# Attention: the third tile's exponentials move between ScalarE's two copies of the values' low rows

## What is computed

```
Q = (query @ Wq.T + bq).reshape(B, Nq, H, D).transpose(0, 2, 1, 3)
K = (key @ Wk.T + bk).reshape(B, Nkv, H, D).transpose(0, 2, 1, 3)
V = (value @ Wv.T + bv).reshape(B, Nkv, H, D).transpose(0, 2, 1, 3)
scores = jnp.einsum('bhqd,bhkd->bhqk', Q, K) * SCALE
scores = scores / temperature
attn = jax.nn.softmax(scores, axis=-1)
out = jnp.einsum('bhqk,bhkd->bhqd', attn, V)
out = out.transpose(0, 2, 1, 3).reshape(B, Nq, C)
return out @ Wo.T + bo
...
x = x + _L0_xattn_ref(_layernorm(x, axis=-1), ctx_1024, ctx_1024, ...)
x = x + _L0_ffn_ref(_layernorm(x, axis=-1), ...)
x = x + _L1_xattn_ref(_layernorm(x, axis=-1), ctx_1024, ctx_1024, ...)
x = x + _L1_ffn_ref(_layernorm(x, axis=-1), ...)
```

## Time and profile before

| | |
|---|---|
| median of 3 runs | 1826.12 us (1825.88 to 1826.61) |
| the profiled execution | 1827.0 us, of which the trace spans 1825.2 us |
| PE, DVE, ACT, POOL busy | 96%, 86%, 67%, 54% of the span |
| granted TensorE clock, mean | 0.987 |

### The profile page before, as it was taken

One profiled execution on the slowest core, in us unless ns is written; L12 is line 12 of the kernel. 1 busy time (PEld: TensorE's weight loads), 2 busy tenths in 40 slices (PEclk: granted clock), 3 DMA queues, 4 the chain that ended last, 5 costly groups with the idle time before them and its releaser, 6 DMA issues.

```text
span 1825.2 us, 29834 instructions
## 1 busy us (share of the span) xinstructions
PE 1748.5 (96%) x9082; PEld 1304.0 (71%) x9162; DVE 1563.2 (86%) x3584; ACT 1223.4 (67%) x3374; POOL 982.1 (54%) x1079
## 2 busy tenths in 40 slices
PE   8898799999999999999889999889999999999997
PEld 7786688888888888888644444457777776767775
DVE  6866789999999999988679888878888988888885
ACT  4575899999999999999533333356656655665543
POOL 2544466666666666666500000156766767767665
PEclk9999999999999999999989999999999999999999
DMA  8666445554455545544379999054445445445311
GB/s 306 201 211 186 105 124 142 153 156 139 139 153 154 146 137 157 154 117 121 93 240 389 407 395 385 26 219 171 167 151 197 161 154 197 153 163 170 124 58 41
DMA packets 153902, 322.08 MB, mean 176 GB/s; under 512 B 47376, under 2 KB 55568, under 8 KB 136080
## 3 DMA queue, kind: packets, MB, share of 16 engines
q1 hardware_dynamic: 153280, 319.38, 53.7%
q10 hardware_dynamic: 464, 0.79, 0.2%
HBM read 163.86 MB, written 105.91 MB: 148 GB/s over the span
## 4 chain that ended last, share of the span: by engine, by line
PE 45%; DVE 2%; issue 1%; ACT 1%; POOL 1%; POOLq 0%; DVEq 0%; ACTq 0%
PE f_pair L1575 12%; PE f_pair L1628 11%; PE f_pair L68 6%; PE f_pair L70 6%; PE f_pair L69 6%; PE f_pair L1615 3%; PE f_pair L1586 1%; ACT f_hf L1696 0%; DVE w L1801 0%; DVE f_st L1833 0%; POOL f_rs L1992 0%; ACT f_room L1671 0%; POOL f_ring L2020 0%; ACT f_hf L1688 0%; DVE f_x2Tl L1821 0%
## 5 line engine op out<-in xcount | busy, mean ns | idle before, releaser
L1320 POOL TENSOR_TENSOR a_pr<-a_pr,a_rcp 128x512 f32<-128x512 f32 x256 | 266.4, 1041 | 262.8 <-DVE a_rcp L1162 262.5
L1070 ACT ACTIVATE a_pr<-a_s,a_nmax 128x128 f32<-128x128 f32 x1024 | 365.4, 385 | 26.9 <-DVE a_nmax L1155 25.1
L1070 ACT ACTIVATION_READ_ACCUMULATOR a_pr<-a_s,a_nmax 128x1 f32 x1024 | 229.3, 224 | 0.0
L1575 PE MATMUL f_pair<-f_room,w 128*128 128x512 bf16 x999 | 225.2, 382 | 2.6 <-ACT f_room L1684 1.3
L1992 POOL TENSOR_TENSOR f_rs<-f_rs,f_half 128x1 f32<-128x1 f32 x128 | 121.2, 947 | 179.2 <-DVE f_rs L1839 179.2
L1793 DVE CUSTOM_DVE_ANT_0 f_hf<-f_pair,nb,sh 128x512 f32<-128x512 f32 x244 | 172.7, 748 | 29.8 <-PE f_pair L1575 29.5
L1575 PEld LDWEIGHTS f_pair<-f_room,w 128*128 128x128 bf16 x1024 | 99.6, 99 | 116.9 <-issue 3.8
L1155 DVE TENSOR_REDUCE a_nmax<-a_s 128x4 f32<-128x512 f32 x256 | 172.0, 672 | 9.6 <-PE a_s L961 7.5
L1170 DVE TENSOR_TENSOR a_pTl<-a_pt,a_pTh 128x512 fp32r<-128x512 f32 x256 | 168.5, 679 | 12.7 <-ACT a_pTh L1082 12.7
L973 PE MATMUL a_pt<-ident,a_pr 128*128 128x128 f32 x1024 | 160.7, 280 | 16.1 <-DVE a_pTl L1170 8.1
L1082 ACT ACTIVATE a_pTh<-a_pt 128x512 fp32r<-128x512 f32 x256 | 151.7, 628 | 4.5 <-PE a_pt L973 4.5
(11 more groups left out here) (443 smaller groups left out, 5091.7 us busy)
## 6 DMA issues: line engine op xcount, KB each, us to landing
hidden<-f_hf SPq DMA_DIRECT2D x57, 1024.0 KB, 8.6
f_hf<-hidden SPq DMA_DIRECT2D x57, 1024.0 KB, 4.8
xr<-x SPq DMA_DIRECT2D x96, 256.0 KB, 3.1
xb<-x SPq DMA_DIRECT2D x16, 1024.0 KB, 5.4
x<-xr SPq DMA_DIRECT2D x64, 256.0 KB, 2.3
ctxh<-bqreph SPq DMA_DIRECT2D x126, 128.0 KB, 2.4
f_room<-x SPq DMA_DIRECT2D x15, 1024.0 KB, 10.3
ctxh<-bqreph SPq DMA_DIRECT2D x128, 64.0 KB, 2.0
```

The lines of the kernel that those rows point to most:

```text
L1070: last = e.activation(pr[:, t, j, :], s_bank[t][:, j * P:j * P + P], ACT.Exp, bias=nmax[kk % 2][:, t, j:j + 1], accum_out=sums[kk % 2][:, ...
L1320: e.tensor_tensor(p, p, rcp[kk % 2][:, t, :].unsqueeze(2).to_broadcast([P, 4, KEYS]), ALU.mult).then_inc(*e_pn)
L1575: last = e.matmul(h_bank[(PAIRS * u + i) % 3][:, q, :], w1[:, k, f * P:f * P + P], xT[u % 2][:, k, :], start=k == 0, stop=k == KC - 1)
```

## The change

ACT takes the exponentials of tile 2 between the two low copies, and no longer behind both. No other engine's order changes, and no wait is added or taken away.

```diff
-            def vlow(b, kk):
+            def vlow(b, kk, i):
                 o = kk - VALUE
                 if not there(b, o):
                     return
                 u = b * TPB + o
-                for i in range(2):
-                    e_pv.wait_ge(e, 2 * u + i)
-                    e_vs.wait_ge(e, 2 * (u - 1) + i)
-                    e.activation(vl[64 * i:64 * i + 64, :], v_bank[i][64 - 64 * i:128 - 64 * i, :], ACT.Copy).then_inc(*e_vl)
+                e_pv.wait_ge(e, 2 * u + i)
+                e_vs.wait_ge(e, 2 * (u - 1) + i)
+                e.activation(vl[64 * i:64 * i + 64, :], v_bank[i][64 - 64 * i:128 - 64 * i, :], ACT.Copy).then_inc(*e_vl)
...
                 qhi(b, kk)
-                vlow(b, kk)
+                vlow(b, kk, 0)
                 exp(b, kk, 2)
+                vlow(b, kk, 1)
                 if not opening:
                     xhi(b, kk)
                 phi(b, kk, 2)
```

## The result

| | before | after |
|---|---|---|
| median of 20 runs each | 1826.0 us (1822.53 to 1829.15) | 1830.62 us (1828.55 to 1835.03) |
| profiled execution, its span | 1827.0, 1825.2 | 1828.84, 1827.0 |
| statistics step, median | 11.24 | 11.48 |
| normalising step, median | 11.24 | 11.23 |
| one of the last steps, median | 10.76 | 10.78 |

The ratio is 1.003, with a 95% interval of 1.0023 to 1.0037: the changed kernel is slower by 5.5 us (4.2 to 6.8). The lengths of steps are the distances between the first maxima of one step and of the next on DVE, worked out from the trace: medians over 24 statistics steps, 25 normalising steps and 4 of the last ones.

A forecast was written before the change was run, and what follows sets the result against it. It took a closed round through PE, ACT, DVE and POOL to bound the kernel, not PE alone. Terms 6.5 + 0.0 + 0.1 - 0.4 = +6.2 us gave 1832.3 us, forecast within 1830.5 to 1834.3, wider range 1827.5 to 1834.8.

The forecast's parts named there:

- The round: Closed round through all four engines sets the 11.24 us step; the change is worth how much `xlo`'s start moves.
- The statistics steps: 26 steps where exponentials would wait for DVE's maxima of tile 2: `xlo` 0.25 later each, 6.5 us.
- The normalising steps: 28 steps where ACT's gained 0.33 is used up by the second copy's new place: 0.00 a step.
- The last steps: Last six or so steps, without `xlo`: ACT's tile 3 exponentials start earlier, gain 0.07 a step, 0.4 in all.
- The late steps: Four steps with late queries' DMA, no gap to fill: two not already counted add 0.6, 0.5 given back, +0.1.
- Overlap for the second copy: Rival: second low copy starts 0.12 earlier, everything behind it 0.15 earlier; -2.1, 1824.0 us; chance 0.06.
- Quick hand-over: Rival: `vsum` 1 starts 0.03 behind the copy, not 0.10, in all 54 steps; +2.4, 1828.5 us; chance 0.04.
- PE the limit: Rival: PE's 96% busy share binds, the round has unseen air, the change does nothing; 1826.1 us; chance 0.05.
- Both together: Rival: second-copy overlap and 0.03 hand-over to `vsum` 1 both hold; -5.9, 1820.2 us, faster; chance 0.02.
- Worse than I say: Rival: no DMA giveback (+0.5), no last-step gain (+0.4), 0.03 more a step (+1.6); 1834.8 us; chance 0.03.
- The signs I named: Statistics step: ACT idle about 0.25, DVE about 0.35, length 11.49; normalising step stays 11.24; PE waits more for POOL.

The follow-up runs named there:

- statistics-only kernel: Changed order in the statistics steps only, old order in normalising steps, against the kernel before: 1830.99 us against 1824.38, ratio 1.0027.
- kernel with less statistics: Changed kernel with one of two statistics instructions left out of every statistics step, against the kernel before: 1825.56 us against 1824.71, ratio 1.0006.
- one wait: Changed kernel with `vsum` 1 no longer waiting for `clo`, only for the low copy, against the kernel before: 1825.55 us against 1824.38, ratio 1.0000.
- the 11.08: Normalising step in us of the kernel before with its second low copy keeping its partitions (own byte tile): 1815.09 us against 1824.71, ratio 0.9958.
- both orders in their places, with one wait less: Changed order in normalising steps only, `vsum` 1 not waiting for `clo`, against the kernel before: ratio 0.9992, rerun 1823.15 us against 1825.82, ratio 0.998.

## Why the prediction was right

I had said 1832.3 us, +6.2. Measured are 1830.62 and +5.5 (4.2 to 6.8).

**The round.** Right. 18.9 us of removed waiting were worth nothing because they lay in a round through PE, ACT, DVE and POOL whose length is set by when `xlo` starts. In a normalising step the exponentials moved up, the second copy moved back behind them, and `xlo` stayed.

**The statistics steps.** The term was 26 x 0.25 = 6.5. The trace has 0.24 in each of the 24 such steps from step 7 on, 5.8, and the statistics-only kernel has 0.23. Each link is within 0.02 of what I worked out: the exponentials 0.03 behind the maxima (0.04 said), the second copy 0.02 behind the read (0.03 said), `vsum` 1 0.10 behind the copy. That it is DVE's own work which makes the loss is shown by the kernel with less statistics. One link of the account was wrong and cost nothing: between `xlo` and the next maxima of tile 2 DVE is not without air, it waits 0.16 for ACT's `phi` 1, before as after. The two other steps lie among the first six of the phase, where the work is another, and they can't be told apart there: those six came out 1.1 shorter in this pair of executions (71.79 and 70.71), and by other amounts in other kernels.

**The normalising steps.** 0.00 said, -0.01 measured, and 0.9996 for the kernel that has only them.

**The last steps.** This term was mis-sized: I said -0.07 a step for six steps, 0.4 in all, and measured +0.02 in the four that nothing disturbs. I had shown no rows for the two figures behind it, 0.14 and 0.11. ACT's exponentials of tile 3 do start earlier, by 0.12 counted from the step's first maxima, but DVE's chain binds now. DVE in one of these steps, before:

```profile
847.92 1.29 DVE L1170 TENSOR_TENSOR a_pTl<-a_pt,a_pTh 128x512 fp32r<-128x512 f32 x2 [0.22 <-ACT a_pTh L1082]
```

After:

```profile
850.73 0.69 DVE L1193 TENSOR_TENSOR a_cs<-a_v,a_vl 64x512 f32<-64x512 f32 x1 [0.44 <-ACT a_vl L1103]
851.45 0.18 DVE L1162 RECIPROCAL a_rcp<-a_sums 128x4 f32<-128x4 f32 x1
851.66 1.29 DVE L1170 TENSOR_TENSOR a_pTl<-a_pt,a_pTh 128x512 fp32r<-128x512 f32 x2
```

After, `plo` 2 starts 0.21 behind the start of `rc` 2, behind its end. In the steps with an `xlo` it starts 0.09 behind it (580.61 to 580.70). `vsum` 1 works on partitions 64 to 127. The next instruction that reads a bank from partition 0 starts 0.03 behind the end of the one ahead of it: elsewhere that is `xlo` (579.97 to 580.00), here it is `plo` 2 (851.63 to 851.66). Before, `plo` 2 waited for ACT's `phi` 2 at that place, and such a hold could not show. I had counted DVE's chain without the 0.12. Without it the step would last some 10.66 and not 10.78 (an estimate), a gain of 0.10. This is read from the rows; no run takes the hold away. By the section "Two Vector instructions with no wait between them" of the Trainium skill's page "VectorE: DVE Perf Modes", such a start waits for all that is ahead of it on VectorE. The trace agrees (0.21 against 0.09), and I should have applied it here as I did on ACT.

Between these and the last normalising step stand three steps that the sum did not have. Two keep 11.24, and step 57 grew by 0.14, as told under the experiments.

**The total.** Counted by steps, the change comes to 26 x 0.24 + 0.14 + 5 x 0.02 - 28 x 0.01 = +6.2 us (an estimate; the timing has 5.5, with 6.2 in its interval). That this meets the forecast's +6.2 is in part luck: the gain of 0.4 that did not come is made up for by 0.01 less in each of 54 steps.

**The late steps.** I said +0.1 for the DMAs. In the trace after, the late steps sum to 3.1 where it was 4.2, as two of the four no longer waited. Since ten other executions have sums from 2.1 to 4.2, this is not the change's doing as far as these runs tell, and 0.1 can be neither confirmed nor refuted.

**The rivals.** *Overlap for the second copy*: refuted, the copy started behind the end of the read; the overlap exists (0.12 ahead of the end) once the copy writes bytes to a tile of its own and keeps its partitions. *Quick hand-over*: not so in the changed kernel, but so in it with one wait. I had priced it at 3.8 us for 54 steps, and with one wait the ratio to before is 1.0000 where the changed kernel's is 1.003. That is 0.3%, with some 0.1% to either side of each; the steps give the 0.07 that was priced. *PE the limit*: refuted by the 11.08. *Both together*: fell with the first two. *Worse than I say*: the +0.4 for the last steps did come (there was no gain), and neither the 0.03 more a step nor, as far as the runs tell, the DMAs' +0.5.

The signs I named were there: ACT idle for 0.27 ahead of the exponentials, DVE for 0.41 ahead of `vsum` 1 (about 0.35 said), the step at 11.48 (11.49 said), and PE waiting for POOL more.

## What to carry to other kernels

A gap on an engine is worth what the next hand-over on the round behind it gains, and it may be what takes up the delays of another engine: follow both reordered instructions to the place where their chains meet again, and do it for each kind of step, because the same exchange was worth 0.00 in one and -0.24 us in the other. A producer whose consumer has no air should not be queued behind work that itself waits for that consumer's engine; here both orders in their places, with one wait less, beat either order throughout by 0.1 to 0.5%. Where an engine's busy share is modelled, look at the distance of two weight loads instead: 0.13 was free and 0.47 was held, both at 96%.

## What the runs showed of the hardware

- **A second wait on one instruction cost time at the hand-over.** From the end of the low copy to `vsum` 1 it is 0.10 with two semaphores and 0.04 with one, though the second had long been satisfied. Over the steps that was 0.06 to 0.07 each.
- **ScalarE held at the low copies that change partitions.** 0.14 on each side of the copy, seen in two kernels that no longer do this: 0.23 to 0.09 behind the read's start, and 0.62 to 0.48 for what follows. Taken out of the kernel before, it shortened every step by 0.14 to 0.16 and the whole by 0.42% (0.27 to 0.57%), more than any order of the instructions did. Tile and type were changed with the partitions, so which of them ends the hold is open. The first low copies, which still change partitions, were held in the same two kernels.
